# Summing heads by 32-column matmuls before one product with Wo, and requesting the next input a step earlier

## The chip, the cores and the metric

The kernel runs on one core of one Trainium2 chip. The metric is device time in microseconds of one execution. The engines are TensorE (PE, with its weight loads PEld), VectorE (DVE), ScalarE (ACT), GpSimd (POOL) and SyncE (SP), which here only issues DMAs.

## The reference

The input is 4 sequences of 1024 tokens with 128 features. One layer of a flow-style linear attention with a GELU feed-forward block is followed by an expert block with low-rank adapters. Cut to the part that the change touches:

```python
q = sigmoid(heads(x @ Wq + bq)); k = sigmoid(heads(x @ Wk + bk)); v = heads(x @ Wv + bv)
# sink_in, src_out, cons_sink, cons_src, src_comp: cumulative sums of q and k along the tokens
qs = q * (sink_in / normal);  vs = v * src_comp
kv = cumsum(k[d] * vs[m])                      # per head, DH x DH = 8 x 8 running sums
out[m] = sum_d qs[d] * kv[d, m] * sink_alloc   # m = 0..7, for each of 16 heads
attn = out.reshape(tokens, 128) @ Wo + bo
h = layernorm(x + attn) * g1 + b1
h = layernorm(h + gelu(h @ W1 + b1_) @ W2 + b2) * g2 + b2_
x2 = layernorm(x + h)
y = layernorm(x2 + gate * experts(x2))         # top 2 of 8 adapters on one shared FFN
```

All arithmetic is fp32.

## The kernel before, in words

The 4096 tokens are 8 tiles of 512 (`TOK`), and a tile is 4 pieces of 128 (`SUB`). Features lie on partitions for q, k, v and their sums (128 = 16 heads x 8). For each m of 0 to 7, SP copies the 16 rows `vs[m::8]` to all 8 rows of their head (`spread_vs`, into `vb`). DVE multiplies by k (`outer_product`, L1005) and sums along the tokens (`cumulate_kv`, L1011), POOL multiplies by the scaled q (`product`, L811, into one of 4 slots of `prod`). PE then does the sum over d and the product with Wo at once (`reduce_out`, L403): four matmuls of 128x128 with the four pieces of `prod` as weights and `s_wor[:, m, :]`, where each row of Wo stands once for every d. They all add into the bank `pO`, which begins with `x + bo` (L399, an identity matmul). The first layer norm reads `pO`: `moments(b, 0)` on DVE, `inverse_std` on POOL, `normalise(b, 0)` on ACT, `h_T` on PE (L411), `h_out` on ACT, and then `hidden` (L420) on PE.

Every engine has its own program, written out by hand, in which one step works on four tiles: a = s + 1 (projections, denominators, first outer products), b = s (outer products 4 to 7, sum over heads, first norm, feed-forward), c = s - 1 (third norm, gate, adapters) and d = s - 2 (rest of the experts, last norm, store). Tile 0 has an `opening`, step 0 is `second_step`, steps 1 to 7 are `step`, and a `closing` follows. Engines are tied by semaphores alone; each works in its written order, so the first instruction that waits holds up everything behind it. Two matmul groups recur below: `head_sums` (L349, on `kq` and on `qk`) sums products of q and k over a head, and `denominators_T` (L356) transposes the denominators for `q_sink` (L944) and `k_src` (L948). `expert_out` is L508, the x transpose `x2_T` L438, the gate's `logits` L444, `inter_base`, `inter1` and `inter2` are L484, L490 and L497.

An fp32 matmul is two MATMUL instructions in the profile, so four matmuls are eight.

Of the kernel before, what the change touches and what calls it, by code (L numbers as in the profile page):

```python
# [9 lines left out]
P = 128  # L10
# [54 lines left out]
def build(nc, x, x_t, att_w, consts, wo_rep, rows, gate_row, ffn_w, moe_w, out):  # L65
    ctx = ExitStack()
    with ctx:
# [12 lines left out]
        s_wor = sb("s_wor", [P, DH, P])  # L80
# [69 lines left out]
        prod = sb("prod", [P, 4, TOK])  # L150

# [87 lines left out]

        kv_ready, cumkv_ready, prod_ready, red_ready = (sem(n) for n in ("kv_ready", "cumkv_ready", "prod_ready", "red_ready"))  # L240
# [34 lines left out]
        def _(sp):  # L275
# [25 lines left out]
            sp.dma_start(s_wor[:, :, :], wo_rep).then_inc(y_free[0], 16)  # L301
# [21 lines left out]
        def _(pe):  # L323
# [70 lines left out]
            def reduce_out(t, m):  # L394

                if m == 0:
                    pe.wait_ge(xbo_ready, t.n + 1)
                    wait(pe, norm_ready[0], SUB * t.n)
                    pe.matmul(pO[:, :], ident, x_bo[:, :, :].rearrange("p s n -> p (s n)"), start=True, stop=False,  # L399
                              skip_group_check=True).then_inc(xadd_done, 1)  # L400
# [129 lines left out]
            def opening(a):  # L530
# [16 lines left out]
                reduce_out(a, 0)  # L547

            def second_step(b):

                a = b.plus(1)
                for m in range(1, 5):
                    reduce_out(b, m)
                head_sums(a, 0, True); head_sums(a, 0, False); project_v(a)
                reduce_out(b, 5)
                denominators_T(a, 0); denominators_T(a, 1)
                reduce_out(b, 6)
                head_sums(a, 1, True); head_sums(a, 1, False)
                reduce_out(b, 7)
                cumulate_e(a); h_T(b); compensation_T(a); factor_T(a)  # L560
# [4 lines left out]
                reduce_out(a, 0)  # L565
# [18 lines left out]
            def step(s):  # L584
# [7 lines left out]
                if A: project_q(a)  # L592
                if B: reduce_out(b, 1)
                if A: project_k(a)
                if D: inter2(d, 2); inter2(d, 3)
                if B: reduce_out(b, 2)
                if C: x2_T(c)
                if B: reduce_out(b, 3); reduce_out(b, 4)
                if C: logits(c)
                if B: reduce_out(b, 5); reduce_out(b, 6); reduce_out(b, 7)  # L600
                if D: expert_out(d, 0)
                if A: head_sums(a, 0, True); head_sums(a, 0, False); project_v(a)
                if D: expert_out(d, 1); expert_out(d, 2)
# [17 lines left out]
                if A: reduce_out(a, 0)  # L621
# [7 lines left out]
        def _(act):  # L629
# [53 lines left out]

            def h_out(t):
# [54 lines left out]
            def second_step(b):  # L739
# [4 lines left out]
                normalise(b, 0)  # L744
# [18 lines left out]
            def step(s):  # L763
# [133 lines left out]
        def _(dve):  # L897
# [263 lines left out]
            def step(s):  # L1161
# [97 lines left out]
```

## Time and profile before

| what | value |
|---|---|
| median of 3 runs | 441.08 us (440.95 to 441.64) |
| profiled execution, its own time | 443.3 us |
| its span | 441.5 us |
| PE busy | 391.1 us, 89% |
| DVE busy | 334.5 us, 76% |
| POOL busy | 224.6 us, 51% |
| ACT busy | 207.4 us, 47% |
| L403 MATMUL, 512 instructions | 72.5 us busy |
| L811 POOL products, 64 | 94.0 us busy |

Times within the trace are microseconds from the span's start. Busy time of PE is modelled: matmuls are pipelined, and an instruction's own duration is longer than the distance to the next. The chain of waits follows back from the last instruction what released each piece; a piece on PE that names PE alone is PE working through its queue. "Granted clock" is the share of full TensorE speed: 1.00 is 2.4 GHz and 0.50 is 1.2 GHz.

### The profile page before, as it was taken

The numbers are of one execution on the slowest core, as the hardware profiler recorded it, in microseconds if no ns is written. First come the engines' busy times: TensorE is split into PE (matmuls) and PEld (weight loads), VectorE is DVE, ScalarE is ACT, GpSimd is POOL, SyncE is SP. The second block draws the span as 40 slices with busy tenths as digits, with TensorE's granted clock in tenths as the row PEclk, the third lists the DMA queues.
The fourth block names the chain that finished last, engine by engine and source line by source line (L and its number), as shares of the span: only waits on it lengthen the run. The fifth ranks groups of instructions, "written<-read, shape, count | busy, mean of one in ns | idle before, by whom it ended". The sixth has DMA issues, their size and how long they took to land.

```text
span 441.5 us, 6398 instructions
## 1 busy us (share of the span) xinstructions
PE 391.1 (89%) x2080; PEld 279.4 (63%) x2080; DVE 334.5 (76%) x795; ACT 207.4 (47%) x375; POOL 224.6 (51%) x263
## 2 busy tenths in 40 slices
PE   8996869488999899899989999999998999889992
PEld 3555766276656767487738775677658775865651
DVE  3549955497779896998789888979799779843532
ACT  2230215334556176437654575537662673275541
POOL 2016224783259435853578329923894368644211
PEclk9888857886999989999899999989999999999997
DMA  8226005400072003700180008200640035000000
GB/s 269 83 59 157 1 1 127 110 2 1 0 172 68 1 0 85 178 1 1 31 221 12 1 2 204 59 0 3 152 111 1 1 84 131 1 1 26 0 25 24
DMA packets 19858, 26.58 MB, mean 60 GB/s; under 512 B 1649, under 2 KB 9969, under 8 KB 19825
## 3 DMA queue, kind: packets, MB, share of 16 engines
q1 hardware_dynamic: 19680, 25.96, 22.8%
q8 instruction: 17, 0.28, 0.3%
q10 hardware_dynamic: 144, 0.21, 0.2%
q14 instruction: 17, 0.13, 0.1%
HBM read 7.29 MB, written 2.10 MB: 21 GB/s over the span
## 4 chain that ended last, share of the span: by engine, by line
PE 42%; DVE 25%; issue 14%; POOL 13%; DMA 3%; ACT 2%; POOLq 0%; DVEq 0%; SPq 0%; ACTq 0%
POOL prod L811 8%; PE pB L349 5%; DVE kv L1005 5%; PE pY L430 5%; PE pG L420 5%; DVE cum_kv L1011 4%; PE pY L508 4%; DMA vb<-vs 3%; PE pG L497 3%; PE pG L490 2%; PE pO L403 2%; DVE cum_ks L901 2%; PE pG L484 2%; DVE cum_q L901 2%; PE pA L337 2%
## 5 line engine op out<-in xcount | busy, mean ns | idle before, releaser
L811 POOL TENSOR_TENSOR prod<-cum_kv,q_fac 128x512 f32<-128x512 f32 x64 | 94.0, 1474 | 34.7 <-DVE cum_kv L1011 28.3
L403 PEld LDWEIGHTS pO<-s_wor,prod 128*128 128x128 f32 x512 | 67.4, 205 | 29.6 <-POOL prod L811 21.5
L403 PE MATMUL pO<-s_wor,prod 128*128 128x128 f32 x512 | 72.5, 294 | 14.1 <-POOL prod L811 13.9
L1005 DVE TENSOR_TENSOR kv<-k,vb 128x512 f32<-128x512 f32 x64 | 53.5, 838 | 7.8 <-DMA vb<-vs 7.8
L798 POOL TENSOR_TENSOR var_eps<-mv,s_con 128x4 f32<-128x4 f32 x32 | 10.0, 312 | 78.6 <-DVE mv L1025 78.6
L1011 DVE TENSOR_TENSOR_SCAN cum_kv<-p_ones,cum_kv,kv 128x512 f32<-128x512 f32 x32 | 40.5, 1275 | 0.6
L1011 DVE TENSOR_TENSOR_SCAN cum_kv<-p_ones,kv 128x512 f32<-128x512 f32 x32 | 38.5, 1214 | 0.5
L508 PEld LDWEIGHTS pY<-s_moe,gel 128*128 128x128 f32 x256 | 33.5, 204 | 6.6 <-issue 4.8
L508 PE MATMUL pY<-s_moe,gel 128*128 128x128 f32 x256 | 34.9, 289 | 0.0
L724 ACT ACTIVATE relu<-pG,s_att 128x512 f32<-128x512 f32 x28 | 19.2, 685 | 33.2 <-PE pG L490 33.1
L430 PEld LDWEIGHTS pY<-s_ffn,gel 128*128 128x128 f32 x256 | 31.0, 193 | 4.4 <-issue 4.4
L420 PE MATMUL pG<-hT,s_ffn 128*128 128x512 f32 x64 | 33.5, 648 | 0.1
L801 POOL TENSOR_TENSOR rstd<-var_eps,s_con 128x4 f32<-128x4 f32 x32 | 32.9, 1027 | 0.0
L430 PE MATMUL pY<-s_ffn,gel 128*128 128x128 f32 x256 | 32.0, 275 | 0.0
L484 PE MATMUL pG<-x2T,s_moe 128*128 128x512 f32 x60 | 30.6, 594 | 0.0
L490 PE MATMUL pG<-u1T,s_moe 128*128 128x512 f32 x60 | 30.5, 593 | 0.0
L497 PE MATMUL pG<-udT,s_moe 128*128 128x512 f32 x60 | 29.5, 605 | 0.0
L1102 DVE SCALAR_TENSOR_TENSOR gel<-pG,neg_bi,relu 128x512 f32<-128x512 f32 x28 | 20.2, 743 | 9.6 <-PE pG L497 9.5
L854 POOL TENSOR_TENSOR e_norm<-esrc,s_con 128x64 f32<-128x64 f32 x8 | 2.8, 345 | 47.4 <-ACT esrc L665 47.4
L702 ACT ACTIVATE ex<-below 128x32 f32<-128x32 f32 x8 | 1.8, 229 | 51.5 <-DVE below L1044 51.5
L693 ACT ACTIVATE gel<-pG,s_att 128x512 f32<-128x512 f32 x32 | 21.9, 684 | 6.2 <-PE pG L420 5.4
L349 PEld LDWEIGHTS pB<-s_att,kq 128*128 128x128 f32 x128 | 16.8, 203 | 12.2 <-issue 8.6
(160 smaller groups left out, 795.8 us busy)
## 6 DMA issues: line engine op xcount, KB each, us to landing
vb<-vs SPq DMA_DIRECT2D x64, 256.0 KB, 4.6
xT<-x_t SPq DMA_DIRECT2D x8, 256.0 KB, 4.8
xt<-x SPq DMA_DIRECT2D x8, 256.0 KB, 5.1
out<-y SPq DMA_DIRECT2D x8, 256.0 KB, 2.3
s_moe<-moe_w SPq DMA_DIRECT2D x1, 836.0 KB, 10.4
s_wor<-wo_rep SPq DMA_DIRECT2D x1, 512.0 KB, 8.2
s_ffn<-ffn_w SPq DMA_DIRECT2D x1, 512.0 KB, 8.8
s_con<-consts SPq DMA_DIRECT2D x1, 502.0 KB, 4.7
```

The lines of the kernel that those rows point to most:

```text
L349: mm = pe.matmul(dst[:, at + s * HEADS:at + (s + 1) * HEADS], src[:, s * P:(s + 1) * P], att("headsum"), start=True, stop=True)
L403: mm = pe.matmul(pO3[:, s, :], prod[:, m % 4, s * P:(s + 1) * P], s_wor[:, m, :], start=False, stop=(m == DH - 1), skip_group_check=True)
L420: pe.matmul(pG[f % 2][:, :], w1[:, f * P:(f + 1) * P], hT[:, :], start=True, stop=True).then_inc(w1_done, 1)
L430: mm = pe.matmul(pY3[:, s, :], gel[:, f, s * P:(s + 1) * P], w2[:, f, :], start=False, stop=(f == FC - 1), skip_group_check=True)
L484: pe.matmul(expert_bank(t, f)[:, :], moe("wi")[:, f * P:(f + 1) * P], x2T[t.par][:, :], start=True, stop=False)
L490: pe.matmul(expert_bank(t, f)[:, :], moe("lb")[:, f * P:(f + 1) * P], u1T[:, :], start=False, stop=True).then_inc(in1_done, 1)
L497: pe.matmul(expert_bank(t, f)[:, :], moe("lb")[:, f * P:(f + 1) * P], udT[:, :], start=False, stop=True, skip_group_check=True).then_inc(i ...
L508: mm = pe.matmul(pY3[:, s, :], hsum[:, f, s * P:(s + 1) * P], wo[:, f, :], start=(f == 0 and s == 0), stop=(f == FC - 1), skip_group_check ...
L801: pool.tensor_tensor(rstd[i][:, :], var_eps[i][:, :], con("mhalf"), ALU.pow).then_inc(rstd_ready[i], 1)
L811: pool.tensor_tensor(prod[:, m % 4, :], cum_kv[t.par][:, m, :], q_fac[t.par][:, :], ALU.mult).then_inc(prod_ready, 1)
L1005: dve.tensor_tensor(kv[:, m % 3, :], k[t.par][:, :], vb[:, m, :], ALU.mult).then_inc(kv_ready, 1)
L1011: dve.tensor_tensor_scan(cum_kv[t.par][:, m, :], scan_ones, kv[:, m % 3, :], start, ALU.mult, ALU.add).then_inc(cumkv_ready, 1)
```

## The change

The product with Wo is taken out of the loop over m. For each m one matmul with 32 weight columns sums the 8 rows of each head (`fold_heads`): the weights are the 128x16 head matrix with 16 zero columns behind it (m < 4) or before it (m >= 4), the output are partitions 32j to 32j + 31 of `pO` with j = m mod 4, and m and m + 4 add into the same 32 partitions. Two m are done in each call. When all eight are in, ACT copies `pO` to `attT` (`attT_out`), and PE writes `x + bo` into `pO` anew and adds four matmuls of `attT` by the reordered Wo (`attn_out`). The norm now waits for `attn_done`. The 512 KB constant `s_wor` becomes the 96 KB `s_fold`. Around it, `fold_heads`, `attn_out`, `h_T` (PE), `attT_out`, `normalise(b, 0)` (ACT) and `moments(b, 0)` (DVE) get new places, and SP requests `xT` of tile s + 2 in step s, behind `spread_vs(a, 1)`, instead of tile s + 1 behind `spread_vs(b, 6)`. Cut to its core:

```diff
-            def reduce_out(t, m):
-                if m == 0:
-                    pe.wait_ge(xbo_ready, t.n + 1)
+            def fold_heads(t, pair):
+                if pair == 0:
                     wait(pe, norm_ready[0], SUB * t.n)
-                    pe.matmul(pO[:, :], ident, x_bo[...], start=True, stop=False, ...).then_inc(xadd_done, 1)
-                pe.wait_ge(prod_ready, DH * t.n + m + 1)
-                for s in range(SUB):
-                    mm = pe.matmul(pO3[:, s, :], prod[:, m % 4, s * P:(s + 1) * P], s_wor[:, m, :],
-                                   start=False, stop=(m == DH - 1), skip_group_check=True)
-                mm.then_inc(red_ready, 1)
+                for m in (2 * pair, 2 * pair + 1):
+                    pe.wait_ge(prod_ready, DH * t.n + m + 1)
+                    j, half = m % 4, m // 4
+                    pe.matmul(pO[32 * j:32 * j + 32, :], s_fold[:, 32 * half:32 * half + 32], prod[:, j, :],
+                              start=(half == 0), stop=(half == 1), skip_group_check=True).then_inc(red_ready, 1)
+            def attn_out(t):
+                pe.wait_ge(attT_ready, t.n + 1)
+                pe.wait_ge(xbo_ready, t.n + 1)
+                pe.matmul(pO[:, :], ident, x_bo[...], start=True, stop=False, ...).then_inc(xadd_done, 1)
+                for s in range(SUB):
+                    mm = pe.matmul(pO3[:, s, :], attT[:, s * P:(s + 1) * P], s_fold[:, 64:64 + P],
+                                   start=False, stop=True, skip_group_check=True)
+                mm.then_inc(attn_done, 1)
...
+            def attT_out(t):                                    # ACT
+                act.wait_ge(red_ready, DH * (t.n + 1))
+                wait(act, attn_done, t.n)
+                act.activation(attT[:, :], pO[:, :], ACT.Copy).then_inc(attT_ready, 1)
...
             def second_step(b):                                 # PE, step 0
-                for m in range(1, 5):
-                    reduce_out(b, m)
+                fold_heads(b, 0); fold_heads(b, 1)
                 head_sums(a, 0, True); head_sums(a, 0, False); project_v(a)
-                reduce_out(b, 5)
                 denominators_T(a, 0); denominators_T(a, 1)
-                reduce_out(b, 6)
+                fold_heads(b, 2)
                 head_sums(a, 1, True); head_sums(a, 1, False)
-                reduce_out(b, 7)
-                cumulate_e(a); h_T(b); compensation_T(a); factor_T(a)
+                fold_heads(b, 3)
+                attn_out(b); cumulate_e(a); h_T(b); compensation_T(a); factor_T(a)
...
             def step(s):                                        # ACT
-                if C: normalise(c, 2); x2T_out(c); gate_exp(c)
-                if A: v_out(a); spread_denominators(a, 0)
+                if C: normalise(c, 2); x2T_out(c)
+                if B: attT_out(b)
+                if C: gate_exp(c)
+                if A: v_out(a); spread_denominators(a, 0); spread_denominators(a, 1)
                 if B: normalise(b, 0)
-                if A: spread_denominators(a, 1)
...
             def step(s):                                        # SP
-                if B: spread_vs(b, 4); spread_vs(b, 5); spread_vs(b, 6)
-                if A and a.n >= 2: load_xT(a)
+                if B: spread_vs(b, 4); spread_vs(b, 5); spread_vs(b, 6); spread_vs(b, 7)
                 if A and a.n >= 1: load_xt(a)
-                if B: spread_vs(b, 7)
                 if A: spread_vs(a, 0); spread_vs(a, 1)
+                if A and 2 <= a.n + 1 < TILES: load_xT(a.plus(1))
                 if D: store(d)
                 if A: spread_vs(a, 2); spread_vs(a, 3)
```

On PE, in a full step, this is what stands around the head sums of tile a before the change (L403 is the sum over heads with Wo, L411 is `h_T`):

```order
L444 MATMUL pM<-s_moe,x2T 128x8 x4
L403 MATMUL pO<-s_wor,prod 128x128 x12
L508 MATMUL pY<-s_moe,gel 128x128 x4
L349 MATMUL pB<-s_att,kq 128x16 x4
L349 MATMUL pB<-s_att,qk 128x16 x4
L337 MATMUL pA<-xT,s_att 128x512
L508 MATMUL pY<-s_moe,gel 128x128 x8
L356 MATMUL pA<-s_con,rden_x 128x128 x4
L508 MATMUL pY<-s_moe,gel 128x128 x4
L411 MATMUL pG<-s_con,n 128x128 x4
L356 MATMUL pB<-s_con,rden_x 128x128 x4
L450 MATMUL pM<-s_moe,x2T 128x128 x4
```

and this stands there after it (lines are those of the changed kernel: L402 is a fold, L409 and L412 are `attn_out`, L350 the head sums, L338 `project_v`, L357 `denominators_T`, L420 `h_T`):

```order
L402 MATMUL pO<-prod,s_fold 32x512 x2
L517 MATMUL pY<-s_moe,gel 128x128 x4
L402 MATMUL pO<-prod,s_fold 32x512 x2
L350 MATMUL pB<-s_att,kq 128x16 x4
L350 MATMUL pB<-s_att,qk 128x16 x4
L338 MATMUL pA<-xT,s_att 128x512
L409 MATMUL pO<-x_bo,s_con 128x512
L412 MATMUL pO<-s_fold,attT 128x128 x4
L517 MATMUL pY<-s_moe,gel 128x128 x8
L357 MATMUL pA<-s_con,rden_x 128x128 x4
L517 MATMUL pY<-s_moe,gel 128x128 x4
L357 MATMUL pB<-s_con,rden_x 128x128 x4
```

The last fold pair stands behind the first `expert_out`, and x and Wo have moved between `project_v` and the other `expert_out`.

On DVE, at the same place, the order before is (`stats<-pO` to `mv<-stats` are `moments(b, 0)`; `rden` are the inverse denominators):

```order
L1040 TENSOR_TENSOR logit<-pM,s_gb 128x32
L928 SCALAR_TENSOR_TENSOR qk<-q,cum_k 128x512
L1042 TENSOR_REDUCE m_log<-logit 128x4
L1021 BN_STATS stats<-pO 128x6 x4
L1023 MEMSET fence 128x1
L1025 BN_AGGR mv<-stats 128x2 x4
L1044 TENSOR_TENSOR below<-logit,m_log 128x32
L933 RECIPROCAL rden<-pB 128x128
L1046 SCALAR_TENSOR_TENSOR pick<-below,s_con 128x32
L940 TENSOR_TENSOR rden_n<-rden,s_con 128x128
```

and after it:

```order
L938 SCALAR_TENSOR_TENSOR qk<-q,cum_k 128x512
L1052 TENSOR_REDUCE m_log<-logit 128x4
L1054 TENSOR_TENSOR below<-logit,m_log 128x32
L1056 SCALAR_TENSOR_TENSOR pick<-below,s_con 128x32
L1058 TENSOR_REDUCE m_pick<-pick 128x4
L943 RECIPROCAL rden<-pB 128x128
L950 TENSOR_TENSOR rden_n<-rden,s_con 128x128
L1031 BN_STATS stats<-pO 128x6 x4
L1033 MEMSET fence 128x1
L1035 BN_AGGR mv<-stats 128x2 x4
L1060 TENSOR_TENSOR first<-pick,m_pick 128x32
```

The moments of `pO` have gone behind the two instructions on the denominators, and three small gate instructions ahead of them.

## Rows read from the trace of the kernel before

**Rows 1.** The page, part 1: busy us (share of the span) xinstructions.

```profile
PE 391.1 (89%) x2080; PEld 279.4 (63%) x2080; DVE 334.5 (76%) x795; ACT 207.4 (47%) x375; POOL 224.6 (51%) x263
```

**Rows 2.** Step 4, window: length, busy (x count) of PE, PEld, DVE, ACT, POOL; clock; DMA.

```profile
225.10:244.70 19.60, 17.49 (x103) 12.65 (x102) 19.29 (x30) 7.68 (x12) 15.14 (x13) 1.00 0.35 90
244.70:249.85 5.15, 5.12 (x40) 4.67 (x41) 3.59 (x18) 2.43 (x7) 1.55 (x4) 1.00 0.01 3
249.85:256.10 6.25, 5.40 (x36) 4.03 (x35) 6.23 (x12) 5.50 (x8) 2.55 (x2) 1.00 0.00 0
256.10:270.95 14.85, 14.83 (x80) 10.34 (x81) 12.46 (x42) 10.33 (x24) 9.05 (x13) 1.00 0.32 75
sum 45.85, PE 42.84 PEld 31.68 DVE 41.57 ACT 25.94 POOL 28.29; mean PE 10.71 PEld 7.92 DVE 10.39 ACT 6.49 POOL 7.07
```

**Rows 3.** Waits of PE, 145 to 380 us: total, times, longest.

```profile
PE pA L327 <- DMA xT<-x_t: 5.2, 4, 1.8
PE pB L349 <- DVE kq L921: 3.9, 5, 0.9
```

**Rows 4.** Chain of waits, 244 to 262 us: start, duration, what.

```profile
243.99 0.61 DVE kq L921
...
244.73 1.93 PE pB L349 x16
246.66 0.95 PE pA L337 x2
247.61 1.78 PE pY L508 x16
...
250.47 1.18 DVE ex L1052
...
256.12 1.07 PE pB L349 x8
...
259.66 0.87 PE pY L426 x2
260.53 0.89 PE pY L430 x8
```

**Rows 5.** Timeline of DVE, step 4: start, duration, instruction, idle before and its releaser.

```profile
245.30 0.88 DVE L1021 BATCH_NORM_STATS2 stats<-pO 128x6 f32<-128x128 f32 x4
...
249.87 0.69 DVE L944 TENSOR_TENSOR q_sink<-q,pA 128x512 f32<-128x512 f32 x1 [1.47 <-PE pA L356]
```

**Rows 6.** Timeline of PE, step 4.

```profile
231.85 1.13 PE L327 MATMUL pA<-xT,s_att 128*128 128x512 f32 x2 [1.44 <-DMA xT<-x_t]
...
240.21 2.92 PE L403 MATMUL pO<-s_wor,prod 128*128 128x128 f32 x24
```

**Rows 7.** Chain of waits, step 7.

```profile
380.94 1.28 POOL prod L811
...
382.26 1.17 PE pO L403 x8
...
383.46 0.89 DVE stats L1021 x4
...
389.64 1.96 PE pG L420 x4
```

**Rows 8.** Timeline of ACT, step 4: a copy out of PSUM.

```profile
237.81 0.60 ACT L698 ACTIVATE x2T<-pM 128x512 f32<-128x512 f32 x1 [0.82 <-PE pM L438]
```

**Rows 9.** Timeline of PE, step 1.

```profile
102.74 2.06 PE L337 MATMUL pA<-xT,s_att 128*128 128x512 f32 x2
106.09 1.12 PE L356 MATMUL pA<-s_con,rden_x 128*128 128x128 f32 x4 [1.29 <-ACT rden_x L648]
```

**Rows 10.** Timeline of PE, step 0.

```profile
59.84 2.08 PE L403 MATMUL pO<-s_wor,prod 128*128 128x128 f32 x8 [0.58 <-POOL prod L811]
```

**Rows 11.** Windows table of PE, step 0: length, busy, granted clock, DMA share, GB/s.

```profile
60.00:64.00 4.00, 2.74 (x13) 0.50 0.02 4
```

**Rows 12.** Timeline of the DMA queue of SP, step 4.

```profile
226.60 1.32 SPq L278 DMA_DIRECT2D xT<-x_t  x1
```

More of the change, by code:

```diff
@@ L62, in run_steps, with build @@
         step(Tile(n))
-def build(nc, x, x_t, att_w, consts, wo_rep, rows, gate_row, ffn_w, moe_w, out):
+def build(nc, x, x_t, att_w, consts, fold_w, rows, gate_row, ffn_w, moe_w, out):
     ctx = ExitStack()
@@ L79, in build @@
         s_con = sb("s_con", [P, 1004])
[L80 removed]
+        s_fold = sb("s_fold", [P, 2 * 32 + P])
         s_row = sb("s_row", [P, 7, P])
@@ L150, in build @@
         prod = sb("prod", [P, 4, TOK])
+        attT = sb("attT", [P, TOK])
         x_bo = sb("x_bo", [P, SUB, P])
@@ L238, in build @@
         compT_ready, vs_ready = sem("compT_ready"), sem("vs_ready")
+        attT_ready, attn_done = sem("attT_ready"), sem("attn_done")
         kv_ready, cumkv_ready, prod_ready, red_ready = (sem(n) for n in ("kv_ready", "cumkv_ready", "prod_ready", "red_ready"))
@@ L564, in second_step @@
                     ffn_out(b, f)
-                reduce_out(a, 0)
             def closing(c):
@@ L591, in step @@
                 if D: inter_base(d, 2); inter1(d, 2); inter_base(d, 3); inter1(d, 3)
-                if A: project_q(a)
-                if B: reduce_out(b, 1)
-                if A: project_k(a)
+                if A: project_q(a); project_k(a)
+                if B: fold_heads(b, 0)
                 if D: inter2(d, 2); inter2(d, 3)
-                if B: reduce_out(b, 2)
                 if C: x2_T(c)
-                if B: reduce_out(b, 3); reduce_out(b, 4)
+                if B: fold_heads(b, 1)
                 if C: logits(c)
-                if B: reduce_out(b, 5); reduce_out(b, 6); reduce_out(b, 7)
+                if B: fold_heads(b, 2)
                 if D: expert_out(d, 0)
+                if B: fold_heads(b, 3)
                 if A: head_sums(a, 0, True); head_sums(a, 0, False); project_v(a)
+                if B: attn_out(b)
                 if D: expert_out(d, 1); expert_out(d, 2)
@@ L605, in step @@
                 if D: expert_out(d, 3)
-                if B: h_T(b)
                 if A: denominators_T(a, 1)
                 if C: lora_in(c)
+                if B: h_T(b)
                 if B: hidden(b, 0); hidden(b, 1)
@@ L743, in second_step @@
                 source_exp(a); alloc_tanh(a)
-                normalise(b, 0)
+                attT_out(b); normalise(b, 0)
                 spread_scale(a, False); spread_scale(a, True)
@@ L1014, in moments @@
                 if i == 0:
-                    dve.wait_ge(red_ready, DH * (t.n + 1))
+                    dve.wait_ge(attn_done, t.n + 1)
                 elif i == 1:
@@ L1172, in step @@
                 if A: q_times_cum_k(a, 0)
-                if C: gate(c, 1)
+                if C: gate(c, 1); gate(c, 2); gate(c, 3); gate(c, 4)
+                if A: inverse_denominators(a); normal_denominators(a)
                 if B: moments(b, 0)
-                if C: gate(c, 2)
-                if A: inverse_denominators(a)
-                if C: gate(c, 3)
-                if A: normal_denominators(a)
-                if C: gate(c, 4); gate(c, 5); sum_exp(c)
+                if C: gate(c, 5); sum_exp(c)
                 if A: sink(a)
@@ L1238 @@
                              np.full((P, SUB), -1.0)], axis=1).astype(np.float32)
-    wo_rep = np.repeat(a["Wo"].reshape(HEADS, 1, DH, P), DH, axis=1).reshape(P, DH, P)
+    none = np.zeros_like(headsum)
+    wo = a["Wo"].reshape(HEADS, 2, 4, P).transpose(2, 1, 0, 3).reshape(P, P)
+    fold_w = np.concatenate([headsum, none, none, headsum, wo], axis=1)
     rows = np.stack([a["bo"], a["ln1_g"], a["ln1_b"], a["b2"], a["ln2_g"], a["ln2_b"], m["bo"]])
@@ L1249 @@
                             m["lora_B"].transpose(0, 2, 1).reshape(P, FF), pieces(m["wo"].T)], axis=1)
-    arrays = {"x": x, "x_t": x.T, "att_w": att_w, "consts": consts, "wo_rep": wo_rep, "rows": rows,
+    arrays = {"x": x, "x_t": x.T, "att_w": att_w, "consts": consts, "fold_w": fold_w, "rows": rows,
               "gate_row": gate_row, "ffn_w": ffn_w, "moe_w": moe_w}
```

8 lines of the change are left out of this document (3 added, 5 removed).

## The prediction, made before the run

> **What bounds the kernel now.** I read the page's busy shares first. TensorE (PE) looks like the bound, busy for 89% of the span against 76% for VectorE (DVE) [rows 1]. That share is a trap here, so the second view is the table of four consecutive stretches of one steady step (s = 4, on chip from 225.1 to 271.0 us, 46 us long) [rows 2]. In the first stretch, 19.6 us long, DVE is busy for 19.29: it runs the last outer products and running sums of tile b, then the two sums of q and k of tile a. PE is busy too, 17.49 us, but it waits at the stretch's end. The reader is to see in the PE waits of steps 2 to 6 that PE stood still for `kq` in all five, 3.9 us together [rows 3]. So PE has finished early each time, and DVE sets the length of this stretch. In the second (5.15 us, PE busy 5.12) the chain of waits runs over PE alone: 16 head-sum instructions 1.93, project_v 0.95, expert_out 1 and 2 1.78, then the transpose for which DVE's `q_sink` waited 1.47 us [rows 4, 5]. The third (6.25 us) is DVE's, up to `qk`. The fourth (14.85 us, PE busy 14.83) is PE's again, beginning with the head sums of `qk` at 256.12 [rows 2, 4]. The period is therefore DVE, PE, DVE, PE in turn, and a microsecond of PE work is worth nothing in the first stretch and a whole one in the second and fourth. All work by Wo (m = 1 to 7) stands in the first stretch, m = 0 and the addition of x behind the end of the fourth: none of it is on the chain in steps 2 to 6.
>
> **The change, part by part.** Two prices recur. A 512-column fp32 matmul (two instructions) takes 0.86 to 0.87 us in a dense row, eight instructions of 128 columns (four matmuls) 0.89 [rows 4].
>
> *The sums over heads.* Per tile, 8 x 0.89 = 7.1 us of `reduce_out` and 0.87 of x become 8 matmuls of 512 columns with 32 columns of weights. No row shows a matmul of such a shape. It streams as many columns as before, so the nearest row is 0.87, that is 7.0 us. Bounds: half, 0.43, if the two of a pair run side by side, and double, 1.7, if narrow weights stream badly. I take 0.87. Either way it lies in DVE's stretch. There PE then has inter_base and inter1 (4 x 0.87), the two projections and two inter2 (4 x 0.87), folds 7.0, four transposes for x2_T 0.45, four narrow matmuls for the logits 0.9 (priced as half of the 16 head-sum instructions), expert_out(0) 0.89: 16.2 us of 19.6, a slack of 3.4. At 0.43 or 0.87 nothing is gained or lost on the chain; at 1.7 it would be 23.1, 3.5 too much. The last fold waits for product 7. The last three reduces ran from 240.21 to 243.13 [rows 6], so that product was there by 242.3, and `kq` is done at 244.60 [rows 4]: one fold fits between.
>
> The Trainium skill ("TensorE: Matmul & The Clock Gate", Part 3, packing small matmuls) has matmuls with 32 weight columns whose outputs lie on different partition groups run at the same time, 2.38 times as fast for three; by that the folds would be near 0.43 each. No run here shows it yet. In the steady steps the sum stays as it is, and in step 0 it would be some 2 us less. "TensorEngine Tiling (Array Packing)", Key Properties, speaks against the change: a switch of tiling mode drains the array. This trace has no such switch. A group that begins after a wait takes 1.17 instead of 0.89 [rows 7]; eight switches per step at that 0.3 are 2.4 us, inside the 3.4 of slack.
>
> *What is new: copy, x, Wo (attT_out, attn_out).* ScalarE (ACT) copies pO in 0.60 us [rows 8]. In steps 2 to 6 head sums and project_v (2.9 us) cover it. But then PE does x (0.87) and four matmuls by Wo (0.89), 1.75 us, between project_v and expert_out(1), in PE's own stretch. `q_sink` moves from 249.87 to about 251.6. Before, `q_sink` could not have come earlier by more than about 0.4, so nothing absorbs it.
>
> *The moments of n1 and h_T.* `moments(b, 0)` stood in a hole of DVE, at 245.30, while it waited for the denominators [rows 5]. It now waits for attn_done, at 247.61 + 1.75 = 249.4 [rows 4]. That still falls in DVE's hole before `q_sink` (queued behind it are gate 5 and sum_exp, 0.3 us). What follows is a serial chain that the last step shows alone: stats at 383.46 to the first `hidden` at 389.64, 6.2 us over DVE, POOL, ACT, PE, ACT [rows 7]. So hidden(b,0) comes at 255.6. The two `hidden` (1.75) and both head sums (1.8) stand behind it in that order and end at 259.2, where before the second head sum ended at 256.12 + 1.07 = 257.19 [rows 4]. That is +2.0 and takes the place of the +1.75, not its side: DVE's qk at about 257.8 is then no longer what comes last. The one microsecond that `ex` (1.18 instead of 0.2) lost beside POOL at 250.47 [rows 4] may vanish, since POOL's h_res now runs later, but it is then likely lost by `kq` or `qk`, and PE's side hides it. Five steps: 5 x 2.0 = 10.0. Bounds 1.4 (all DVE stalls gone, a chain faster by its waits) to 2.6.
>
> *Step 1* has no expert work. PE waited 1.29 us for the copy of the denominators [rows 9]. At half clock, which project_v at 102.74 shows (2.06 against 1.1), attn_out is 3.6 us, and hidden(b,0) comes at 104.7 + 3.6 + 6.5 = 115 where it began at 110.95; at full clock it is +1.4. Between 1.4 and 3.9 I take 3.0.
>
> *Step 0* runs PE at clock 0.50 [rows 11]. The last reduce began at 59.84 and took 2.08 [rows 10]. Now fold 6 begins when the head sums end (59.2), fold 7 behind it, then the copy, x and Wo: at half clock 59.2 + 3.4 + 0.65 + 3.5 = 66.8 against 61.9, at full clock 63.3. The pair 4, 5 stands ahead of head sums there and may add 1.8. Between 1.4 and 6.7 I take 4.5; behind attn_out the cumulate_e of the next tile waits too.
>
> *Step 7*: the chain goes product 7, reduce 1.17, stats [rows 7]. Now fold 1.0, copy 0.65, x 0.87, Wo 0.89 + 0.17: 3.65, less 1.17 = +2.5, with no cover, since the end follows from it.
>
> *xT a step ahead.* PE waited for xT 5.2 us in steps 2 to 6 [rows 3], 1.44 of it at 231.85 [rows 6]. It lies in DVE's stretch, where PE has slack, so 0. Its request costs SP 1.32 us [rows 12] and now stands between vb 1 and the store. The store waits there anyway, so vb 2 leaves no later. Steps 0 and 1 have no store, and vb 2 comes 1.3 us later there, with some 1.5 us in hand. Cost 0, bound 0.5 a step. The smaller constant load ends long before its first use.
>
> *Sum*: 10.0 + 3.0 + 4.5 + 2.5 = +20.0 us. The profiled execution took 443.3 for a span of 441.5, 2.2 above the median of 441.08; the addition holds for either. 441.1 + 20 = **461 us**.
>
> **Rivals.** *A, faster: PE is the bound.* For it: PE is busy for 89% of the span. If pairs overlap fully, PE sheds per tile 7.1 - 3.5 - 0.89 = 2.7 us plus about 0.7 for xT, 8 x 3.4 = 27, at best 414; half of it on the chain gives 428. It decides from the point at which PE ends the first stretch later than DVE. Against it: five waits for `kq` out of five. *B, hidden:* attn_out falls into a hole, should the copy of the denominators be what PE waits for; only step 7 (2.5) and the low bound of step 0 (1.4) cost: 441 + 4 = 445. Against it: PE was busy 5.12 of 5.15. *C, the clock:* PE idles longer in DVE's stretch, and 32-column weights may keep the clock lower. In step 0, where PE idles often, it is at 0.50 [rows 11]. If PE's second stretch (now 6.9 us) ran at half clock for about half its length in each of steps 2 to 6, that is +3.4 each, 17 more: 478. It decides only if low stretches come in nearly all steps. Narrow matmuls at 1.7 end at the same place (5 x 3.2).
>
> **Numbers.** Forecast (chain lengthened at attn_out, 453 to 468) 0.80, A 0.08, B 0.03, C 0.09. For 8 in 10 I go from 451 to 470. About 0.2% is what a measurement of this kernel can tell from no change: faster by more 0.09, within 0.02, slower by more 0.89.
>
> **What would show it.** In steps 2 to 6 of the new profile: PE waits before `kq` longer than the 0.8 us of now (3 or more if pairs overlap); `q_sink` waits for its transpose about 3 us minus the moments; x and Wo take 1.75 between project_v and the expert; step 4 about 48 us long instead of the 45.85 of the four stretches [rows 2]; the fold's rows 0.87 apart (0.43 if side by side). Wrong if PE no longer waits for `kq`, if the period stays, or if long stretches of steps 2 to 6 are granted half the clock, where the four stretches here show 1.00.

## The result, and the profile after

| | before | changed |
|---|---|---|
| median | 441.01 us (438.79 to 441.64, 4 runs) | 465.74 us (461.51 to 471.73, 4 runs) |
| profiled execution | 443.3 us, span 441.5 | 471.73 us, span 469.9 |
| mean granted clock, 145 to 385 us of the trace | 0.97 | 0.92 |

The changed kernel is slower by the ratio 1.0475 (95% interval 1.0413 to 1.0537), predicted 461 us, range 451 to 470. The four runs of the changed kernel lie at 461.5 (two) and at 469.9 and 471.7; the ratio is made from the first two, of which there is no trace, and the trace below is of the slowest. A second trace (467.66 us, called "the repeat" from here) therefore stands beside it wherever a size matters. Against the kernel before, the first trace is 28.4 us longer and the repeat 24.4.

The page of the changed kernel: busy time of each engine, and the fold's group (busy us, mean ns of one, idle time before).

```profile
PE 399.7 (85%) x1760; PEld 236.2 (50%) x1760; DVE 338.0 (72%) x795; ACT 212.8 (45%) x383; POOL 227.8 (48%) x263
...
L402 PE MATMUL pO<-prod,s_fold 128*32 128x512 f32 x128 | 54.4, 725 | 12.5 <-POOL prod L821 12.5
```

PE has 320 instructions fewer than in [rows 1] and is busy 8.6 us longer. The 72.5 us of work by Wo in 512 instructions became 54.4 of folds in 128 and Wo once per tile, so instructions that the change doesn't touch must have got slower: that is the first hint of the clock.

Where the 28.4 us went is read off one mark that every step has, the running sum `cum_q` on DVE. Its first start shown is of step 1, the second of step 2, the last of step 6. Before:

```profile
97.35 1.20 DVE L901 TENSOR_TENSOR_SCAN cum_q<-p_ones,q 128x512 f32<-128x512 f32 x1
...
145.16 1.26 DVE L901 TENSOR_TENSOR_SCAN cum_q<-p_ones,cum_q,q 128x512 f32<-128x512 f32 x1
...
333.16 1.26 DVE L901 TENSOR_TENSOR_SCAN cum_q<-p_ones,cum_q,q 128x512 f32<-128x512 f32 x1
```

After:

```profile
101.10 1.20 DVE L911 TENSOR_TENSOR_SCAN cum_q<-p_ones,q 128x512 f32<-128x512 f32 x1
...
151.46 1.26 DVE L911 TENSOR_TENSOR_SCAN cum_q<-p_ones,cum_q,q 128x512 f32<-128x512 f32 x1
...
353.34 1.26 DVE L911 TENSOR_TENSOR_SCAN cum_q<-p_ones,cum_q,q 128x512 f32<-128x512 f32 x1
```

| part | before | changed | added | added in the repeat |
|---|---|---|---|---|
| opening and step 0 | 97.35 | 101.10 | 3.75 | 0.6 |
| step 1 | 47.81 | 50.36 | 2.55 | 2.75 |
| four periods, steps 2 to 5 | 188.0 | 201.88 | 13.9 | 14.35 |
| step 6 from its mark, step 7, closing | 108.3 | 116.6 | 8.2 | 6.7 |

So the steady step grew by 3.5 us (13.9 / 4; 3.6 in the repeat) where 2.0 was forecast. The base of that difference is firm to some 0.4 us per step: four periods take 187.9 us in the trace of b_warm (below), whose steps 2 to 6 are those of the kernel before, and 186.6 in that of e_xt. The timeline of PE in step 4 of the changed kernel (start, time, instructions; in brackets the wait before and for whom) shows what stands there:

```profile
242.41 1.05 PE L402 MATMUL pO<-prod,s_fold 128*32 128x512 f32 x4
243.39 1.98 PE L506 MATMUL pG<-udT,s_moe 128*128 128x512 f32 x4
247.27 0.65 PE L447 MATMUL pM<-s_con,x 128*128 128x128 f32 x4 [1.90 <-ACT x L685]
...
256.63 1.04 PE L350 MATMUL pB<-s_att,kq 128*128 128x16 f32 x8 [1.96 <-DVE kq L931]
257.52 1.04 PE L350 MATMUL pB<-s_att,qk 128*128 128x16 f32 x8
258.41 1.10 PE L338 MATMUL pA<-xT,s_att 128*128 128x512 f32 x2
259.35 1.81 PE L409 MATMUL pO<-x_bo,s_con 128*128 128x512 f32 x2
260.95 1.92 PE L412 MATMUL pO<-s_fold,attT 128*128 128x128 f32 x8
262.66 2.05 PE L517 MATMUL pY<-s_moe,gel 128*128 128x128 f32 x16
...
269.08 1.98 PE L429 MATMUL pG<-hT,s_ffn 128*128 128x512 f32 x4 [0.87 <-ACT hT L696]
```

Three things are to be seen. A pair of folds, four instructions and two 512-column matmuls, is over 0.98 us after it began (242.41 to 243.39): the two run side by side. (The last four folds of the tile do not: each starts when its own product arrives, so all eight take 5.5 us of PE in this step, not 3.9.) PE then waits 1.90 for the third norm and 1.96 for `kq`; before, the `kq` wait was 0.8 [rows 3], and PE waited for the third norm only once, 1.4 us in step 7. And x and Wo (L409, L412) are there between project_v and the expert, but x takes 1.60 to the next start and Wo 1.71, where the dense rows of before have 0.87 and 0.89 [rows 4]. The granted clock from 258.5 to 262.7 is 0.61 on average; head sums and the expert around it run at full speed.

The waits of PE from 150 to 400 us of the changed kernel (us, times, longest), beside [rows 3]: the wait for xT is gone, `kq` has grown, and the norm's last link is new.

```profile
PE pM L447 <- ACT x L685: 10.4, 5, 2.2
PE pB L350 <- DVE kq L931: 7.6, 4, 2.0
PE pG L429 <- ACT hT L696: 4.3, 5, 0.9
```

The chain of waits in the same step, to be read against [rows 4]. It no longer leaves PE for DVE's `q_sink` and `ex`; it goes on through Wo into the norm and back to PE at `hidden`, 6.2 us later (262.91 to 269.08), as step 7 of before had alone [rows 7].

```profile
261.16 1.72 PE pO L412 x8
...
262.91 0.89 DVE stats L1031 x4
...
269.08 1.98 PE pG L429 x4
```

DVE in that stretch, to be read against [rows 5]: it stands 3.02 us for Wo, and `q_sink` still waits 0.80.

```profile
262.91 0.89 DVE L1031 BATCH_NORM_STATS2 stats<-pO 128x6 f32<-128x128 f32 x4 [3.02 <-PE pO L412]
...
265.19 0.69 DVE L954 TENSOR_TENSOR q_sink<-q,pA 128x512 f32<-128x512 f32 x1 [0.80 <-PE pA L357]
265.79 0.20 DVE L1062 SCALAR_TENSOR_TENSOR ex<-first,ex 128x32 f32<-128x32 f32 x1
...
267.79 1.61 DVE L931 SCALAR_TENSOR_TENSOR kq<-k,cum_qs 128x512 f32<-128x512 f32 x1
```

Step 7, the chain, against [rows 7]. The last product ends at 406.45, the stats begin 3.83 us later; before it was 1.24 (382.22 to 383.46). That is +2.6.

```profile
406.50 1.06 PE pO L402 x2
407.58 0.61 ACT attT L691
408.23 1.13 PE pO L409 x2
409.36 0.91 PE pO L412 x8
410.28 0.89 DVE stats L1031 x4
```

Steps 0 and 7 again, timeline of PE. In step 0 x and Wo run at half clock (the fold pairs before them too); in step 7 the eight `hidden` instructions take 5.64, where they take 4.05 in the repeat and in the kernel before. In the repeat step 7's `hidden` runs at full clock, and so do x and Wo of step 0.

```profile
58.29 2.57 PE L402 MATMUL pO<-prod,s_fold 128*32 128x512 f32 x4
61.55 2.07 PE L409 MATMUL pO<-x_bo,s_con 128*128 128x512 f32 x2 [0.69 <-ACT attT L691]
63.41 1.77 PE L412 MATMUL pO<-s_fold,attT 128*128 128x128 f32 x8
...
416.45 5.64 PE L429 MATMUL pG<-hT,s_ffn 128*128 128x512 f32 x8 [0.87 <-ACT hT L696]
```

### The profile page after: what moved, and what is told of

Its sections match the earlier page's. It is cut to its first block, busy times and chain, and to the rows that moved or that the text cites. A ratio compares the mean times of both kernels' runs of the same rounds, so it can differ in the third digit from the quotient of the medians.

```text
span 469.9 us, 5781 instructions
## 1 busy us (share of the span) xinstructions
PE 399.7 (85%) x1760; PEld 236.2 (50%) x1760; DVE 338.0 (72%) x795; ACT 212.8 (45%) x383; POOL 227.8 (48%) x263
## 4 chain that ended last, share of the span: by engine, by line
PE 48%; DVE 24%; issue 12%; POOL 8%; ACT 4%; DMA 3%; SPq 0%; POOLq 0%; DVEq 0%; ACTq 0%
PE pG L429 7%; PE pB L350 7%; DVE kv L1015 6%; DVE cum_kv L1021 6%; PE pY L439 5%; DVE stats L1031 3%; PE pG L506 3%; DMA vb<-vs 3%; POOL prod L821 3%; PE pO L409 3%; PE pG L499 3%; POOL rstd L811 2%; PE pG L493 2%; PE pY L517 2%; PE pO L412 2%
## 5 line engine op out<-in xcount | busy, mean ns | idle before, releaser
L402 PE MATMUL pO<-prod,s_fold 128*32 128x512 f32 x128 | 54.4, 725 | 12.5 <-POOL prod L821 12.5
L429 PE MATMUL pG<-hT,s_ffn 128*128 128x512 f32 x64 | 35.8, 688 | 6.1 <-ACT hT L696 6.1
L517 PEld LDWEIGHTS pY<-s_moe,gel 128*128 128x128 f32 x256 | 31.8, 197 | 9.5 <-issue 7.8
L350 PEld LDWEIGHTS pB<-s_att,kq 128*128 128x128 f32 x128 | 18.1, 213 | 24.6 <-issue 21.8
L685 ACT ACTIVATE n<-pO,shift,rstd 128x128 f32<-128x128 f32 x32 | 12.0, 456 | 34.9 <-POOL shift L814 34.9
L350 PE MATMUL pB<-s_att,kq 128*128 128x16 f32 x128 | 18.3, 276 | 10.6 <-DVE kq L931 10.6
L1031 DVE BATCH_NORM_STATS2 stats<-pO 128x6 f32<-128x128 f32 x32 | 7.1, 286 | 27.1 <-PE pO L412 27.1
L691 ACT ACTIVATE attT<-pO 128x512 f32<-128x512 f32 x8 | 4.8, 597 | 47.3 <-PE pO L402 47.3
```

The costliest lines, as they stand in the source:

```text
L350: mm = pe.matmul(dst[:, at + s * HEADS:at + (s + 1) * HEADS], src[:, s * P:(s + 1) * P], att("headsum"), start=True, stop=True)
L402: pe.matmul(pO[32 * j:32 * j + 32, :], s_fold[:, 32 * half:32 * half + 32], prod[:, j, :], start=(half == 0), stop=(half == 1), skip_group ...
L429: pe.matmul(pG[f % 2][:, :], w1[:, f * P:(f + 1) * P], hT[:, :], start=True, stop=True).then_inc(w1_done, 1)
L517: mm = pe.matmul(pY3[:, s, :], hsum[:, f, s * P:(s + 1) * P], wo[:, f, :], start=(f == 0 and s == 0), stop=(f == FC - 1), skip_group_check ...
```

## Experiments

The theory has three parts: added PE work costs its own length only in PE's stretch and nothing in DVE's; the order (Wo behind the value projection, the norm chain behind Wo) is what costs, not the folding; and a part of the loss is half clock. The runs take them in turn. Sets run together share the runs of the kernel before; its medians were 440.86, 441.49, 440.34 and 441.29 us.

**e_p1: the kernel before, 1.75 us more PE work in PE's stretch.**

```diff
                 if A: head_sums(a, 0, True); head_sums(a, 0, False); project_v(a)
+                if A and D: pe.wait_ge(hsum_ready, FC * (d.n + 1)); fill(pG[1], 2)    # 2 matmuls of 512 columns, steps 2 to 6
                 if D: expert_out(d, 1); expert_out(d, 2)
```

> The kernel before, with two identity-free 512-column fp32 matmuls on a constant (1.74 us, results unused) between project_v and expert_out(1) in steps 2 to 6. My theory (this stretch belongs to PE): every step grows by 1.4 to 1.75, together 7 to 9 us, so 448 to 450. Rival (PE is not what is waited for there, or the waits absorb it): under 2 us.

Measured 450.66 us (449.43 to 452.19) against 440.86, ratio 1.0234 [1.0190, 1.0277]: +9.8, 1.96 per step. PE's stretch has no cover. The fillers themselves ran partly at half clock (248.31 to 251.10, 2.79 for 1.75), so even this plain insertion does not stay at full clock, and the 1.96 is work and clock together. PE's waits for `kq` were no longer than before (0.58 to 0.95): the clock can fall there without a lengthened wait.

**e_d1: the kernel before, the same work in DVE's stretch, and xT a step ahead.**

```diff
                 if A: project_k(a)
+                if A and D: pe.wait_ge(udT_ready, c.n); fill(pM, 2)
                 if D: inter2(d, 2); inter2(d, 3)
```

> The kernel before, with the same two matmuls (1.74 us) behind project_k in steps 2 to 6, in DVE's stretch, and xT requested a step ahead so that PE's wait for xT makes room. My theory: DVE sets this stretch, so the change is within 1 us of none, 440 to 442. Rival A (PE is the bound by its 89%): 5 x 1.74 less the 5 us of waits for xT, at least +4.

**e_xt: the kernel before, only xT a step ahead** (the diff of SP's program alone).

> The kernel before with nothing but the request of xT a step ahead. My theory: 0, within 0.5 us of 441.0, since the wait for xT lies in DVE's stretch. Rival A (PE bound): the 5 us of PE's waits come back, 436.

e_d1 measured 440.46 us, ratio 0.9989 [0.9964, 1.0014]; e_xt 440.93 us, 0.9996 [0.9970, 1.0022]. 1.75 us of PE work per step is free in DVE's stretch and costs 1.96 in PE's, and the removal of 5.2 us of waits for xT gives nothing. These three runs settle the first part.

**f_wide: the changed kernel with 128 weight columns per fold.** Each fold then fills the whole array and nothing runs side by side; arithmetic and order are the same.

```diff
-                    pe.matmul(pO[32 * j:32 * j + 32, :], s_fold[:, 32 * half:32 * half + 32], prod[:, j, :],
-                              start=(half == 0), stop=(half == 1), ...)
+                    pe.matmul(pO[:, :], s_fold[:, m * P:(m + 1) * P], prod[:, m % 4, :],
+                              start=(m == 0), stop=(m == DH - 1), ...)
```

> The changed kernel, with 128 weight columns per fold (the head matrix at columns 16m to 16m + 15, zeros elsewhere) in place of 32, so that all eight folds add into the whole bank and no two can run side by side. The folds then cost 6.9 us per tile instead of the 3.5 seen. Theory 1 (their place has slack, and a busier PE keeps its clock): same or faster than the changed kernel, 455 to 462, and a granted clock above 0.91. Rival (the short folds were a gain that hides a larger loss): 3 us or more slower than the changed kernel's 461.5, so 465 or above.

Measured 466.91 us (466.63 to 467.85), ratio 1.0601 [1.0565, 1.0637]. That misses the forecast of 455 to 462 by 5 us and lies where the rival had it, 465 or above. But both were set against the 461.5 us runs; the changed kernel measured again has 466.71 us and a ratio of 1.0559 [1.0509, 1.0609] (a_again, below), and the two can't be told apart. Its PE timeline in step 4:

```profile
238.43 1.88 PE L401 MATMUL pO<-prod,s_fold 128*128 128x512 f32 x4
240.15 1.88 PE L505 MATMUL pG<-udT,s_moe 128*128 128x512 f32 x4
...
255.48 1.72 PE L408 MATMUL pO<-x_bo,s_con 128*128 128x512 f32 x2
257.00 1.91 PE L411 MATMUL pO<-s_fold,attT 128*128 128x128 f32 x8
```

A pair takes 1.72 to the next start instead of 0.98. Over the whole program the folds keep PE busy for 68.6 us instead of 54.4, 1.8 us more per tile, and the time is that of the repeat: folding's speed is worth nothing. Half clock between the head sums and the expert is there too, in four of the steps 2 to 6, so it does not need 32-column weights. In step 3 it is absent, although PE had waited 1.75 us for `kq`.

**f_early: the changed kernel, Wo ahead of the head sums, the moments ahead of the denominators.** Now PE waits for the copy where it would have waited for `kq`.

```diff
                 if B: fold_heads(b, 3)
+                if B: attn_out(b)
                 if A: head_sums(a, 0, True); head_sums(a, 0, False); project_v(a)
-                if B: attn_out(b)
...
                 if C: gate(c, 1); gate(c, 2); gate(c, 3); gate(c, 4)
+                if B: moments(b, 0)
                 if A: inverse_denominators(a); normal_denominators(a)
-                if B: moments(b, 0)
```

> The changed kernel, with attn_out one place earlier on PE in steps 1 to 7, ahead of the head sums of tile a instead of behind project_v, and moments(b, 0) on DVE ahead of the inverse denominators, where it was before the change. No work is added or taken. The copy attT is ready at 255.3 while PE stands still until kq at 256.5. Theory 1 (the loss is attn_out's place in PE's stretch and the norm's chain behind it): head sums begin 0.5 to 0.7 later than kq, and 2 to 3 us per step come back, so 446 to 453. Rival 2 (the loss is the cost of the folds, the switches of tiling or the copy themselves, wherever attn_out stands): within 2 us of the changed kernel, 460 or more.

Measured 454.69 us (451.21 to 456.30), ratio 1.0302 [1.0253, 1.0352]: 12 of the 25 us come back by two moved calls, at the same arithmetic. Its PE timeline in step 4:

```profile
238.05 0.66 PE L447 MATMUL pM<-s_con,x 128*128 128x128 f32 x4 [2.02 <-ACT x L685]
...
247.59 1.12 PE L409 MATMUL pO<-x_bo,s_con 128*128 128x512 f32 x2 [0.73 <-ACT attT L691]
...
249.44 0.96 PE L350 MATMUL pB<-s_att,kq 128*128 128x16 f32 x8
```

No wait for `kq` is left; the half-clock stretch (0.53 from 239.0 to 245.5) has moved forward into DVE's stretch, behind the wait of 2.02, where PE has slack. Four steady periods are 191.2 us (188.0 before), so the steady loss is 0.8 per step; the rest sits in the opening with step 0 (+4.1) and in the tail (+5.5), and step 1 is 1.8 shorter. 454.69 is slightly above the 446 to 453 that I gave and well under the rival's 460.

**f_busy: the changed kernel, PE kept busy in both waits**, by two 512-column matmuls of no use ("fillers") before x2_T and two before the head sums, steps 2 to 6.

```diff
+                if A and D: pe.wait_ge(udT_ready, c.n); fill(pM, 2)
                 if C: x2_T(c)
...
                 if B: fold_heads(b, 3)
+                if A and D: pe.wait_ge(q_ready, a.n + 1); fill(pA, 2)
                 if A: head_sums(a, 0, True); head_sums(a, 0, False); project_v(a)
```

> The changed kernel with two idle-filling 512-column matmuls on a constant ahead of x2_T and two ahead of the head sums in steps 2 to 6, where PE waits 1.9 and 2.0 us. Theory of the clock (the half clock at x and Wo, 1.65 and 1.72 us instead of 0.87 and 0.89, comes from PE's waits and the narrow folds before it): x and Wo return to full clock, 1.5 us less per step, 453 to 458, granted clock above 0.92. Rival (the clock falls for the narrow head sums and not for the waits): no lower than 461.

**a_again: the changed kernel unchanged**, on the same chip.

> The changed kernel again, on the same chip as the others, to have its fast and low-clock runs beside theirs. Expected: 461 to 472, as before.

f_busy measured 458.93 us (6 runs: one at 452.02, five from 458.86 to 461.92; too scattered for an interval of the ratio), a_again 466.71 us (463.85 to 471.21, 6 runs), ratio 1.0559 [1.0509, 1.0609]. The two sets do not overlap: with 3.5 us more matmuls per step the kernel's median is 7.8 us lower. f_busy's median is 0.9 above the 453 to 458 that I gave and under the rival's 461. The two windows rows (length, busy times with counts, granted clock) over 145 to 385 us, of the repeat and of f_busy:

```profile
145.00:385.00 240.00, 217.32 (x1048) 137.62 (x1045) 196.85 (x474) 125.70 (x225) 131.40 (x149) 0.92 0.21 52
```

```profile
145.00:385.00 240.00, 230.81 (x1110) 137.23 (x1110) 208.32 (x486) 131.42 (x238) 141.55 (x160) 1.00 0.24 58
```

And the same place on PE, step 4, of the repeat and of f_busy:

```profile
252.39 1.04 PE L350 MATMUL pB<-s_att,kq 128*128 128x16 f32 x8 [1.95 <-DVE kq L931]
...
254.96 2.05 PE L338 MATMUL pA<-xT,s_att 128*128 128x512 f32 x2
256.81 1.92 PE L409 MATMUL pO<-x_bo,s_con 128*128 128x512 f32 x2
258.52 1.83 PE L412 MATMUL pO<-s_fold,attT 128*128 128x128 f32 x8
260.19 1.95 PE L517 MATMUL pY<-s_moe,gel 128*128 128x128 f32 x16
```

```profile
254.38 1.04 PE L350 MATMUL pB<-s_att,kq 128*128 128x16 f32 x8
...
257.10 1.02 PE L409 MATMUL pO<-x_bo,s_con 128*128 128x512 f32 x2
257.96 1.05 PE L412 MATMUL pO<-s_fold,attT 128*128 128x128 f32 x8
258.85 1.95 PE L517 MATMUL pY<-s_moe,gel 128*128 128x128 f32 x16
```

From the head sums to the expert it is 7.80 us in the repeat, 6.03 in the first trace of the changed kernel and 4.47 in f_busy, with equal instructions. What differs is the granted clock and what PE did before: it stood 1.95 and 1.96 us for `kq` in the first two and ran matmuls in the third. The same stretch in each of the steps 2 to 6, from the timelines (e_p1 has its fillers in the place of x and Wo, e_late two reduces):

| trace | waits for `kq`, us | head sums to expert, us |
|---|---|---|
| changed | none, 1.83, 1.96, 1.83, 1.95 | 4.61, 7.62, 6.03, 7.79, 7.79 |
| repeat | 0.54, 1.83, 1.95, 1.83, 1.95 | 4.47, 7.79, 7.80, 7.79, 7.79 |
| f_busy | none | 4.47 five times |
| f_wide | 1.77, 1.75, 1.77, 1.75, 1.87 | 6.16, 4.47, 5.94, 7.78, 7.79 |
| e_p1 | 0.95, 0.82, 0.58, 0.82, 0.94 | 4.44, 6.13, 6.13, 7.48, 6.13 |
| e_late (below) | 3.90, 2.88, 2.36, 3.32, 3.28 | 8.57, 7.79, 7.80, 7.80, 7.80 |

Four steady periods take 193.7 us in f_busy, 48.4 each: at full clock the changed step costs 1.4 us more than before, so half clock adds the other 2.1. The table gives nearly the same by another way: over 4.47, the four stretches that lie in the counted periods lose 8.2 us in the changed kernel, 2.0 per step, and 10.0 in the repeat, 2.5. Filling the two waits thus takes the half clock away in all five steps. The length of the wait for `kq` alone does not tell when it comes: f_wide was at full clock once after 1.75 us, and e_p1 at half clock four times after waits under 1 us.

**e_norm: the kernel before, only the later places of the first norm** (moments behind the denominators, `h_T` behind lora_in, `normalise` behind both spreads).

> The kernel before with only the moved places of the first norm: moments(b, 0) behind the denominators on DVE, both copies of the denominators ahead of normalise(b, 0) on ACT, h_T behind lora_in on PE. My theory: the stats come at 247.9 instead of 245.3, hidden(b,0) at 254.1 instead of 252.3, the second head sum 0.4 us later: +0.3 to +0.8 per full step, 442 to 446. Rival (the norm's place alone is the loss): 10 us or more.

Measured 447.28 us (446.40 to 448.79), ratio 1.0140 [1.0095, 1.0185], 1 us above the range given. By its `cum_q` marks step 1 lost 2.1 us of it and the steady period only 0.3. The moved places alone are cheap as long as the sum over heads is done early.

**e_late: e_norm, and the last two reduces (1.78 us) moved from ahead of the head sums to behind project_v.** No fold, no copy, no narrow weights: the old arithmetic with the changed kernel's order.

```diff
-                if B: reduce_out(b, 5); reduce_out(b, 6); reduce_out(b, 7)
+                if B: reduce_out(b, 5)
                 if D: expert_out(d, 0)
                 if A: head_sums(a, 0, True); head_sums(a, 0, False); project_v(a)
+                if B: reduce_out(b, 6); reduce_out(b, 7)
```

> The kernel before, with the moved norm of the earlier run (447.3) and besides the last two reduces, 1.78 us, between project_v and expert_out(1) in steps 1 to 7, the place and the length of attn_out. No fold, no copy, no narrow weights; the product with Wo is as before. Theory (place of the last PE work and the norm's chain behind it): 1.75 to 2.0 per full step by the prediction's sum, 1 to 2 more where the clock halves, as in the changed kernel: 453 to 461. Rival (half or more of the loss is the folds', the copy's or the switches' own): 450 or less.

Measured 469.86 us (467.73 to 471.29), ratio 1.0632 [1.0577, 1.0686]: upward out of my range, and no faster than the changed kernel (466.71, with intervals of the ratio that overlap). PE in step 4:

```profile
257.50 1.36 PE L349 MATMUL pB<-s_att,kq 128*128 128x16 f32 x8 [2.36 <-DVE kq L921]
...
262.25 3.21 PE L403 MATMUL pO<-s_wor,prod 128*128 128x128 f32 x16
265.30 1.95 PE L508 MATMUL pY<-s_moe,gel 128*128 128x128 f32 x16
```

The 1.78 us that left DVE's stretch reappear as wait for `kq` (2.36 instead of 0.8), and the stretch behind it runs at half clock: 7.80 us for 4.5 us of work. The steady step grew by 4.6 us (206.4 against 188.0 over four). This shows the order to be enough for the whole loss. I had priced a step at 1.75 to 2.0 plus 1 to 2 for the clock; by the table above the stretch lost 3.5 per step to half clock, the other 1.1 being work and chain, and step 1 alone grew by 5.2. So it was again the clock that I priced too low.

**f_order: f_early with h_T and normalise back at their old places. f_order_busy: that, with two fillers before x2_T.**

> The kernel with attn_out ahead of the head sums (the earlier run of 454.7), and besides h_T ahead of denominators_T(a, 1) on PE and normalise(b, 0) between the two copies on ACT, as they stood before the change. Theory (the norm's chain behind attn_out is the rest of the step's loss, as PE waited 0.87 us for hT in each of five steps): hidden(b,0) comes 0.5 to 0.9 earlier, so 2 to 5 us less, 450 to 453. Rival (attn_out's own 1.75 us are all that is left, the order of the norm costs nothing now): 454 to 456.

> The same, with two idle-filling 512-column matmuls on a constant ahead of x2_T in steps 2 to 6, where PE waits 2 us for the third norm. Theory of the clock: the half clock at logits, fold 4 to 7 and expert_out (1.88, 1.92, 2.08 us for what takes 0.9 to 1.0 at full clock) goes; it lies mostly in DVE's stretch, so 1 to 4 us less than without, 447 to 451. Rival (no clock effect or wholly hidden): within 1 us of the one without.

f_order measured 457.20 us (451.77 to 460.11), ratio 1.0344 [1.0293, 1.0396], no gain over f_early: my theory fell, and the rival (454 to 456) came nearer. PE no longer waits for `hT` (4.3 us in f_early), but for `qk` one group later:

```profile
259.40 1.07 PE L350 MATMUL pB<-s_att,qk 128*128 128x16 f32 x8 [0.81 <-DVE qk L939]
```

f_order_busy measured 453.12 us (450.67 to 458.67), 1.0274 [1.0229, 1.0320]. The intervals of the two overlap, and the traces speak against a gain where the fillers are: four steady periods take 191.2 us in f_early, 191.5 in f_order and 191.2 in f_order_busy. The fillers took the half clock out of DVE's stretch (mean of 145 to 385 us 0.96 instead of 0.93), but in four steps some 3 us of it came later instead (0.50 from 258 to 260 us, for one), so this run does not price the half clock in DVE's stretch.

**b_warm: the kernel before, 13 fillers in the waits of steps 0 and 1**, where its granted clock is low [rows 11].

```diff
+                fill(pY, 3)                        # step 0, ahead of reduce 1
+                fill(pY, 1)                        # ahead of reduce 6
-                cumulate_e(a); h_T(b); compensation_T(a); factor_T(a)
+                cumulate_e(a); fill(pY, 2); h_T(b); compensation_T(a); factor_T(a)
+                fill(pM, 4)                        # ahead of tile 1's first reduce
...
+                if s.n == 1: fill(pM, 2)           # behind project_q
+                if s.n == 1: fill(pM, 1)           # behind reduce 2
```

> The kernel before with 13 filling matmuls of 0.87 us on a constant in steps 0 and 1 alone, each placed where PE waits for products or the norm (three ahead of reduce 1, one ahead of reduce 6, two ahead of h_T, four ahead of tile 1's first reduce, two and one in step 1). Theory of the clock: PE at 0.50 from 52 to 70 us and from 101 to 111 us comes from those waits; with them filled 3 to 6 us less, 435 to 438. Rival (the narrow matmuls set the clock there, and the fillers only add): 441 or more.

Measured 439.12 us (436.20 to 441.15, 12 runs) against 440.34 (17 runs), ratio 0.9972 [0.9946, 0.9998]. The clock of 40 to 72 us is 0.79, against 0.63 in the trace of the kernel before; but e_late, whose program is unchanged up to there, has 0.74, so only a part of the rise is the fillers'. The 435 to 438 us that I expected did not come. It is the only version whose interval lies below the kernel before, by 0.3%, and it barely excludes no change.

## Why the prediction held, and which term was off

The ratio puts the changed kernel at 462 us, and 461 was forecast. The direction and the mechanism were right; that the number came so close is partly luck: it rests on two runs without a trace, the medians of four and of six runs are 465.7 and 466.7, and in both traces the largest term of the sum is off in two ways that partly cancel.

- **DVE's stretch absorbs the folding: right.** A fold was priced at 0.87. A pair whose products are ready is over in 0.98, 0.49 each, against 1.72 a pair in f_wide; the last four folds of a tile come one at a time. The Trainium skill ("TensorE: Matmul & The Clock Gate", Part 3) says that 32-column matmuls on different partition groups run together; the trace agrees. The Trainium skill ("TensorEngine Tiling (Array Packing)", Key Properties) has a switch of mode drain the array. Here a pair costs 0.98 to the next start where a single matmul of 512 columns costs 0.86, so I estimate both switches together at no more than 0.12 us, not the 0.3 each that I allowed. Neither mattered: f_wide has the same time.
- **xT ahead gives 0: right** (e_xt), and the `kq` wait grew as said, from 0.8 to 1.96.
- **The norm chain takes the place of attn_out: right.** The chain of waits runs 262.91 to 269.08 through it, the 6.2 us that step 7 had shown. The stall of `ex` beside POOL left (0.20) and came to `kq` (1.61), as expected.
- **Step 7: +2.5 forecast, +2.6 measured.** Step 1: 3.0 forecast, 2.55 and 2.75 measured. **Step 0: 4.5 forecast, 3.75 and 0.6 measured**; in the repeat x and Wo of step 0 ran at full clock, which the lower bound of 1.4 had stood for. A part of this is scatter: up to the same mark, traces with an unchanged step 0 (e_p1, e_late, e_norm) take 96.0 to 97.9 us.
- **Steps 2 to 6: 2.0 per step forecast, within 1.4 to 2.6; 3.5 measured. This is the mis-sized term.** It has two errors of opposite sign. At full clock the step costs 1.4 (f_busy), the low bound, not 2.0. And some 2.1 more is half clock in the stretch from the head sums to Wo: 4.47 us of work became 6.03 and 7.80 in step 4. I had this as rival C, at 3.4 per step on top of the forecast (461 + 17 = 478) and a chance of 0.09, as something that comes in nearly all steps or not at all. It came in four of five, in the stretch that I had named, at some two thirds of that size; the sum itself had no term for it. Of the two causes that I named, the narrow weights are not needed (f_wide and e_late have the low clock without them), and PE's idling in DVE's stretch has a part in it, since f_busy, which fills that, has full clock.
- **My own sign of being wrong came.** I had said that long stretches of steps 2 to 6 at half the clock would show me wrong. They came, 3 to 7 us in a row. And step 4, the only one that I had read, was not typical: in the kernel before, the granted clock falls in steps 2, 3, 5 and 6 too (0.50 from 164 to 166, 212 to 214 and 294 to 296 us, 0.52 from 342 to 344), which is why its mean is 0.97 and not 1.00.
- The books of the first trace: against the forecast, step 0 -0.75, step 1 -0.45, steps 2 to 6 +7.5 (5 x 1.5), step 7 +0.1, and +1.6 for `hidden` of step 7 at half clock, that is +8.0 of the 28.4 - 20.0 = 8.4. The fifth steady period is taken equal to the other four here. 0.4 us are in no term.
- **Rivals A and B fell:** PE sheds time in DVE's stretch (the folds of step 4 take 5.5 us where the reduces took 7.1, and the wait for xT is gone) and the kernel is slower, not 428; the work is not hidden, not 445.

Left open: what else decides when the clock falls, since e_p1 lost it after short waits and f_wide kept it once after a long one; how the 461.5 us runs divide over the steps, and so whether the steady step is 3.5 us longer there too (between the two traces the steady periods agree to 0.5 us, and 3.15 of the 4.0 us between them lie in the opening and step 0); and which link keeps f_order from gaining. That the stall of `ex` leaving is why full clock costs 1.4 and not 1.75 was argued, not tried.

## What to carry to other kernels

For every instruction added or moved on an engine, ask first in whose stretch it lands: the same 1.75 us cost 0 in DVE's stretch and 1.96 in PE's, and 1.8 us per tile of saved PE work in a stretch with slack were worth nothing. Work taken out of slack is not harmless either: it opens a wait, and here, in four of five steps, the granted clock fell to half within 3 us behind a wait of 2 us, in the very stretch that sets the end. Read the clock of every step of the trace, not of one. If a new serial tail cannot be avoided, put it where its engine waits anyway (two moved calls gave back 12 of 25 us), and price the clock for every stretch behind a wait that the change lengthens.

## What the runs showed of the hardware

Two fp32 matmuls of 32 weight columns and 512 columns of data, on different partition groups of the output, took 0.98 us together to the next start, where two of 128 weight columns took 1.72. TensorE at 1.2 GHz nearly doubled x (0.86 to 1.60 and 1.71) and Wo (0.89 to 1.71 and 1.67) in the middle of a stretch in which it had no idle time at all; the stretch followed a wait of 1.96 and 1.95 us. Adding 3.5 us of matmuls with no use per step raised the mean granted clock of 145 to 385 us from 0.92 to 1.00 and lowered the median by 7.8 us. Two elementwise DVE instructions of 0.2 and 0.7 us took 1.2 and 1.6 us when a POOL instruction ran beside them (`ex` in [rows 4] beside POOL's `h_res` from 250.33 to 251.61, `kq` above beside the `h_res` that began at 267.58).
